# The second low half of each expert on VectorE, and another order of loads and weights around the end of the first expert layer

## What is computed

```python
x = x + _L0_xattn_ref(_layernorm(x), ctx_1024, ctx_1024, mask, wq, wk, wv, wo)  # 16 heads
x = x + _L0_ffn_ref(_layernorm(x), wr, w1, b1, w2, b2)
#     h = _gelu(jnp.einsum('ecd,edf->ecf', xg, w1) + b1[:, None, :])   # 256 -> 1024
#     y = jnp.einsum('ecf,efd->ecd', h, w2) + b2[:, None, :]           # 1024 -> 256
#     wy = y * g[..., None];  summed back to the tokens
x = x + _L1_xattn_ref(_layernorm(x), ctx_1024, ctx_1024, mask_BxS)    # one head of 256, no projections
x = x + _L1_ffn_ref(_layernorm(x), gate_w, w1, w2, w3)                # silu(x w1) * (x w3), then w2
```

## Time and profile before

| | us |
|---|---|
| median of 3 runs | 1095.21 (1092.34 to 1095.92) |
| the profiled execution, its own time | 1098.09 |
| its span, first to last instruction | 1095.9 |
| PE busy in the span | 939.3 (86%) |
| DVE, ACT, POOL busy | 682.5, 545.6, 480.0 |

### The profile page before, as it was taken

The page is one execution under the profiler, slowest core; times in us unless marked ns, Lnnn a source line. Parts: engine busy times, 40 slices in busy tenths (PEclk is TensorE's granted clock), DMA queues, the critical chain, the costliest instruction groups (busy, mean ns, idle before and its releaser), DMA issues. The chain is left out here.

```text
span 1095.9 us, 22844 instructions
## 1 busy us (share of the span) xinstructions
PE 939.3 (86%) x7879; PEld 853.7 (78%) x7879; DVE 682.5 (62%) x1931; ACT 545.6 (50%) x1208; POOL 480.0 (44%) x462
## 2 busy tenths in 40 slices
PE   5889998998899839999999936872799999999997
PEld 4778877877787629898889914662799999999977
DVE  5556565675566557666666625756567777778533
ACT  3778877887788725555555513430234333433221
POOL 2123134142413235666666731356354565456423
PEclk9999998999999859999999968985799999999999
DMA  7878787886576047667766686642543453345101
GB/s 187 172 204 207 184 201 190 222 202 146 148 171 156 28 129 216 166 173 171 172 173 165 137 205 158 179 151 89 191 116 84 114 145 101 101 114 135 18 7 22
DMA packets 110020, 160.22 MB, mean 146 GB/s; under 512 B 11584, under 2 KB 98976, under 8 KB 107968
## 3 DMA queue, kind: packets, MB, share of 16 engines
q1 hardware_dynamic: 95952, 140.16, 48.9%
q0 software_dynamic: 13936, 18.33, 8.3%
HBM read 103.45 MB, written 56.96 MB: 146 GB/s over the span
## 5 line engine op out<-in xcount | busy, mean ns | idle before, releaser
L312 PE MATMUL ps<-XGH,WH 128*128 128x280 f32 (+1 forms) x768 | 223.0, 290 | 16.3 <-ACT GT L836 12.3
L312 PE MATMUL ps<-XGL,WH 128*128 128x280 f32 (+1 forms) x768 | 222.2, 289 | 0.0
L312 PE MATMUL ps<-XGH,WL 128*128 128x280 f32 (+1 forms) x768 | 221.7, 289 | 0.0
L1595 POOL TENSOR_TENSOR HTL<-GT,HTH 128x280 fp32r<-128x280 f32 x128 | 132.9, 1062 | 165.9 <-DVE HTH L1335 165.9
L1207 DVE CUSTOM_DVE_ANT_0 NS<-ps,negm 112x375 f32<-112x375 f32 x256 | 138.0, 545 | 108.4 <-PE ps L418 96.6
L312 PEld LDWEIGHTS ps<-XGH,WH 128*128 128x128 f32 x768 | 148.3, 193 | 21.4 <-ACT GT L836 17.0
L764 ACT ACTIVATE PP<-NS,MN 112x375 f32<-112x375 f32 x256 | 156.4, 611 | 3.2 <-DVE MN L1207 2.7
L312 PE MATMUL ps<-WH,HTH 128*128 128x256 f32 (+1 forms) x536 | 152.4, 284 | 2.0 <-DVE YY L1350 2.0
L426 PE MATMUL ps<-cst,PP 112*125 112x112 f32 x768 | 138.9, 291 | 17.4 <-ACT PP L764 14.5
L312 PE MATMUL ps<-WL,HTH 128*128 128x256 f32 (+1 forms) x536 | 150.5, 281 | 0.0
L312 PE MATMUL ps<-WH,HTL 128*128 128x256 f32 (+1 forms) x536 | 149.9, 280 | 0.0
(11 more groups left out here) (211 smaller groups left out, 1881.7 us busy)
## 6 DMA issues: line engine op xcount, KB each, us to landing
WG<-in_v SPq DMA_DIRECT2D x48, 512.0 KB
KST<-k_scratch SPq DMA_DIRECT2D x48, 376.0 KB, 5.5
WG<-in_w SPq DMA_DIRECT2D x32, 512.0 KB
k_scratch<-KHL SPq DMA_DIRECT2D x64, 188.0 KB
CT<-in_ctx_t SPq DMA_DIRECT2D x32, 375.0 KB, 7.0
xg_scratch<-zero SPq DMA_DIRECT2D x8, 1289.8 KB, 10.3
xg_scratch<-zero SPq DMA_DIRECT2D x16, 586.2 KB, 9.0
XG<-xg_scratch SPq DMA_DIRECT2D x14, 536.0 KB, 3.7
```

Of the source, the lines that this page charges most:

```text
L312: m = e.matmul(out_ap, l, r, start=n == 0, stop=n == len(steps) - 1)
L1595: e.tensor_tensor(HTL[:, f, cols], GT[:, gi % 3, :], HTH[:, f, cols], ALU.subtract).then_inc(hl_pool[layer], 1)
```

## The change

Five edits, all in the order of work or in who does it; what is computed stays the same.

1. **The low half of unit gi = 1 of each expert**, in both layers, is made by DVE: `by_pool(gi)` is true for odd gi except where gi % 16 is 1, and `hl_of` counts by it.
2. **The last block of layer 0** (n = 39, expert 7, c = 4, 48 rows) goes into the first `GT` buffer rather than into `YY`, and no longer waits for the transfer of block 35.
3. **Weights behind rows in layer 0's last expert**: the two pieces of weights 38 and 39 are made after the five blocks on ACT, DVE and POOL, rather than before or between them. Their next loads (pieces 42 and 43, 512 KB each) leave the boundary and go to the start of layer 1's `sp_experts`, behind its first rows.
4. **Contexts ahead of the wait**: SP issues `ctx_t` 2 and 3 and `ctx_n` 1 before it waits for layer 0's adds, and loads the last eight batches of `X` as two pieces of four, with `ctx_n` 2 and 3 between the pieces.
5. **Clears**: expert 3 issues two of the clears, experts 4 to 6 one each, expert 7 none.

```diff
-XLOADS = ((0, 2), (2, 4), (4, 8), (8, B))
+XLOADS = ((0, 2), (2, 4), (4, 8), (8, 12), (12, B))
...
+        def row_block(layer, n):
+            GT, YY = ebufs[layer][5:7]
+            r = rows_of(n % 5)
+            return GT[0:r, 0, 0:D] if (layer, n) == (0, 5 * E - 1) else YY[0:r, n % NY, :]
...
+        def by_pool(gi):
+            return gi % 2 == 1 and gi % 16 != 1
+
         def hl_of(gi):
-            return gi // 2 + 1, (gi + 1) // 2
+            pool = sum(by_pool(i) for i in range(gi + 1))
+            return gi + 1 - pool, pool
...
-                if gi % 2 == 0:
+                if not by_pool(gi):
                     e.wait_ge(hh[layer], gi + 1)
                     e.tensor_tensor(HTL[:, f, cols], g, HTH[:, f, cols], ALU.subtract).then_inc(hl_dve[layer], 1)
...
-                    if n >= NY:
+                    if NY <= n < 5 * E - 1:
                         e.wait_ge(*row_done(0, n - NY))
-                    e.tensor_tensor(YY[0:r, n % NY, :], ps[0:r, 4 + n % 2, 0:D], B2[0:r, u, :], ALU.add).then_inc(y_out[0], 1)
+                    e.tensor_tensor(row_block(0, n), ps[0:r, 4 + n % 2, 0:D], B2[0:r, u, :], ALU.add).then_inc(y_out[0], 1)
...
-                    if c < per - 2 and last:
-                        lo(base + per * ex + 10 + c)
                     rows_done(ex, c)
                     if c < per - 2 and not last:
                         lo(base + per * ex + 10 + c)
+                for c in range(per - 2 if last else 0):
+                    lo(base + per * ex + 10 + c)
```

ACT and POOL have the same move of their weights behind the five blocks. On SP:

```diff
+            if layer == 1:
+                for c in range(2):
+                    sp_chunk(e, 4 * E + 10 + c)
...
                 if layer == 0:
-                    cleared_rest(ex)
+                    for rest in (ex,) if ex < 3 else (3, 4) if ex == 3 else (ex + 1,):
+                        if rest < E:
+                            cleared_rest(rest)
...
                 for c in range(5):
-                    if c < per - 2:
+                    if c < per - 2 and not (layer == 0 and ex == E - 1):
                         sp_chunk(e, base + per * ex + 14 + c)
...
             e.wait_ge(y_mm[0], 5 * E)
             context_n(0)
-            for n in range(5 * E - NY, 5 * E):
-                e.wait_ge(*row_done(0, n))
-            kept(0)
-            kept(1)
             context_t(e, 2)
             context_n(1)
-            kept(2)
             context_t(e, 3)
+            for n in range(5 * E - 1 - NY, 5 * E):
+                e.wait_ge(*row_done(0, n))
+            for i in range(3):
+                kept(i)
             context_n(2)
             kept(3)
             context_n(3)
+            kept(4)
```

More of the change, by code:

```diff
@@ L538, in rows_out @@
                 if c in (0, 2):
-                    by_dve, by_pool = hl_of((ex * 2 + c // 2) * 8 + 7)
-                    e.wait_ge(hl_dve[layer], by_dve)
-                    e.wait_ge(hl_pool[layer], by_pool)
+                    n_dve, n_pool = hl_of((ex * 2 + c // 2) * 8 + 7)
+                    e.wait_ge(hl_dve[layer], n_dve)
+                    e.wait_ge(hl_pool[layer], n_pool)
                 pairs = []
@@ L830, in activated @@
                 if gi >= 3:
-                    by_dve, by_pool = hl_of(gi - 3)
-                    e.wait_ge(hl_dve[layer], by_dve)
-                    if by_pool:
-                        e.wait_ge(hl_pool[layer], by_pool)
+                    n_dve, n_pool = hl_of(gi - 3)
+                    e.wait_ge(hl_dve[layer], n_dve)
+                    if n_pool:
+                        e.wait_ge(hl_pool[layer], n_pool)
                 if layer == 0:
@@ L843, in rows_gated @@
                 r = rows_of(c)
-                y = YY[0:r, n % NY, :]
+                y = row_block(0, n)
                 e.wait_ge(y_out[0], n + 1)
@@ L862, in act_experts @@
                 last = layer == 0 and ex == E - 1
-                for c in range(per - 2 if last else 0):
-                    act_weights_hi(e, base + per * ex + 10 + c)
                 for c in range(5):
@@ L872, in act_experts @@
                         act_weights_hi(e, n)
+                for c in range(per - 2 if last else 0):
+                    act_weights_hi(e, base + per * ex + 10 + c)
                 if between and ex == E - 2:
@@ L1609, in rows_added @@
                     out_offset=bass.IndirectOffsetOnAxis(ap=XG[0:rows_of(c), ex % 2, c, RW_ID:RW_ID + 1].bitcast(I32), axis=0),
-                    in_=YY[0:rows_of(c), n % NY, :], in_offset=None, bounds_check=T - 1, oob_is_err=False,
+                    in_=row_block(layer, n), in_offset=None, bounds_check=T - 1, oob_is_err=False,
                     compute_op=ALU.add).then_inc((d_add0, d_add)[layer][n % NY], 16)
@@ L1618, in pool_experts @@
                     for f in range(8):
-                        if f % 2:
+                        if by_pool((ex * 2 + hf) * 8 + f):
                             halves_lo((ex * 2 + hf) * 8 + f)
```

2 lines of the change are left out of this document (1 added, 1 removed).

## The result

The changed kernel takes 1083.4 us (median; 1081.1 to 1086.4) where the kernel before takes 1095.4 beside it (1092.3 to 1095.9). The ratio of the times is 0.988, with an interval of 0.985 to 0.991: faster by 9 to 16 us. The prediction was 1080, with a range of 1071 to 1090.

What follows compares the result with a forecast made beforehand. PE was taken to wait for ACT in layer 0's experts, then for adds and transferred bytes around the layer boundary. Gains 6.7 + 2.8 + 5.8 = 15.3 us, from the median 1095.21 to 1079.9; range 1071 to 1090.

Steps and rivals of the forecast that it cites:

- Low half: Layer 0's experts: PE's waits at unit 8 go, 0.35 us stays in each of six experts; gain 7.45 us.
- 555.16 plus 0.8: Expert 5, layer 0: POOL's adds end at 555.16, its low half of unit 3 takes 0.8, so ends at 556.0.
- Double clear: Expert 3, layer 0: 1.29 MB more pass while adds are in flight; cost 0.7 us, bounds nothing and about 4.5.
- the bank wait of 0.65: End of layer 0: DVE no longer makes weights ahead of block 35, freeing PE's bank; 0.65 us of PE's time.
- End of layer 0: Weights leave the front of POOL's adds, last block doesn't wait 5.13; X's loads go out earlier; 2.8 us in all.
- Contexts ahead: Second attention: three of nine contexts move ahead of the wait, fewer bytes before batch 4's scores; gain 5.8 us, 3.4 wait stays.
- rival C: Layer boundary: batch 4's context lands first, the hole closes, the last add lands in 3.8; 1074.4 us, chance 0.14.
- A: Layer 0's experts: PE's wait only moves to unit 12, layer 0 gives 2; 1084.6 us, chance 0.16.
- B: Second attention: bound by transfers further on, gives the contexts' gain back; 1085.7 us, chance 0.13.
- D: Layer boundary: four contexts hold SP, X's loads queue behind, batch 4's scores 4.3 late; 1092.8 us or slower, chance 0.04.
- E: Whole kernel: A and B together, the change does next to nothing; 1090.4 us, chance 0.07.

Runs made afterwards that it cites:

- the split: Each ctx_n loaded by two transfers (partitions 0 to 111 and 112 to 124) instead of one: ratio to before 0.9829 in the changed kernel, 0.9873 in the kernel before.
- the two runs on the low half: Kernel before with only unit 1's low half moved to VectorE: ratio to before 0.9938; changed kernel with that edit undone: 0.9928.

## Why the prediction was right, and where not

The forecast of 15.3 us lies inside the measured 9 to 16, at its upper end. Part of that is luck: in the traces layer 0's experts gave 3.6 where the terms have 7.35, and the end of the layer and the second attention gave more than their terms, so that errors of 3 to 4 us stood against each other. And the term of the contexts has about the right number by a reason that doesn't hold. The terms one by one:

**Low half: 7.45 predicted, some 6.5 by the times of two runs, 5.1 and 6.2 in their traces.** The mechanism was right to the unit: the waits at unit 8 are gone, and the next ones stand behind POOL's low halves of units 3 and 5. The size was a little off, since 0.35 was left for each expert and 1.0 stayed. Here is why, in the timelines of ACT, DVE and POOL at the start of expert 2 in the changed kernel:

```profile
479.78 0.88 ACT L847 ACTIVATE GT<-ps,B 128x280 f32<-128x280 f32 x2 [1.74 <-POOL HTL L1606]
...
482.10 1.11 ACT L847 ACTIVATE GT<-ps,B 128x280 f32<-128x280 f32 x2 [1.44 <-POOL HTL L1606]
...
478.03 1.96 DVE L1349 TENSOR_TENSOR HTL<-GT,HTH 128x280 fp32r<-128x280 f32 x1
479.91 0.29 DVE L1346 CAST HTH<-GT 128x280 fp32r<-128x280 f32 x1
...
477.47 1.37 POOL L1618 DMA_INDIRECT x_scratch<-YY,XG  x1 [0.30 <-issue]
478.40 1.27 POOL L1606 TENSOR_TENSOR HTL<-GT,HTH 128x280 fp32r<-128x280 f32 x1
...
480.28 1.70 POOL L1606 TENSOR_TENSOR HTL<-GT,HTH 128x280 fp32r<-128x280 f32 x1 [0.61 <-DVE HTH L1346]
```

The step that failed is "555.16 plus 0.8". The last add in the earlier trace rows runs until 555.60 (554.23 + 1.37), and POOL's first low half behind it ended at 556.4, 0.8 later, with DVE idle. In the changed kernel it is the same: the last add ends at 478.84 (477.47 + 1.37), the low half of unit 3 at 479.67. So that one was due at 556.4 and not at 556.0, which is about the 0.32 that PE waits at unit 10. The second wait has another source. In the same moments DVE made the low half of unit 4, which took 1.96 in place of 0.45; its cast of unit 5 began only at 479.91, and POOL, free at 479.67, waited 0.61 for it (the last row).

The prediction set the Trainium skill's rule (SBUF — State Buffer, Who interferes with whom: a VectorE instruction with two SBUF inputs and a GpSimd instruction that reads SBUF exclude each other) at up to 0.9 for each expert, and then left it out because the new low half falls while POOL issues adds. That was right for the new one in this expert, which took 0.45 beside an add's issue, like the one at 471.28 above, but the rule came in where a later low half of DVE's meets POOL's first. The trace agrees with the rule, and here it was DVE that paid: POOL's low half ended no later behind the add than with DVE idle (0.83 against 0.80). In layer 1's experts little changed (0.7 us less), as predicted.

**Double clear: 0.7 predicted, about 4.5 measured** (217.7 against 213.2 with one clear in each). This is the one term that was plainly mis-sized. The sentence "adds landed nearly in time elsewhere, so I take 0.7" is the step: 4.5 was the bound, from the row with 5.13, and that row was the nearest one in kind, since it too had a clear in flight with an expert's adds. The wait measured was 5.14. The times of that pair differ by only 1.6, uncertain by 4, so the 4.5 are the traces'. Layer 0's experts in sum: 7.35 predicted with the bank wait of 0.65, 3.6 in the trace.

**End of layer 0: 2.8 predicted (0.65 of it inside the experts), 3.3 and 0.6 in the trace, but not for the reasons given.** All that the prediction described took place: no wait of the last block, POOL's adds in a row, the last one ended 4.8 us after PE's end. But undoing edits 2 and 3 lost nothing that can be measured, and putting the clear back into expert 7 didn't delay X's issue either. Either is enough, and the prediction credited the first and counted the second only as bytes. What it left out is a price of edit 4: the contexts ahead of the wait hold the last add back by 1.8 us (4.2 from its issue to X's, 2.4 with them behind).

**Contexts ahead: 5.8 predicted; 4.3 to 5.9 by times, 6.8 from X's issue to the scores of batch 4.** The number holds and its reason doesn't. I divided bytes by the rate of the earlier trace rows and took that rate for a limit of the transfers. Splitting one narrow load raised it from 192 to 224 GB/s, and to 264 with the contexts behind the wait. The gap closed wholly, as in rival C, where 3.4 was to stay, partly because X's first rows landed 2.5 us later and took PE's other work along. That the granted clock stays at 0.50 for 3.4 to 4.5 us behind a gap of 9 us, as three traces show, was in no term; half the work of these microseconds makes it some 2 us more (an estimate). The prediction quoted the Trainium skill (DMA: Bandwidth & Descriptors, Why a DMA increments its semaphore by 16 and not by 1), by which a load over 125 partitions runs on 5 engines and one over 112 on 16, and then used it for a difference of one microsecond. No trace here shows single engines, but two things agree with it. The engines' busy share goes from 0.77 to 1.01 by the split, and the stretches at 0.33 or 0.34, which go with it, are what 5 engines of 16 would give where all give 1.10 (an estimate from that rule and the windows above: 1.10 x 5/16 = 0.34). It should have been asked what the same sentence says of the hole itself.

**The rivals.** A is ruled out by the two runs on the low half. B is partly true: the values' waits nearly doubled, but the whole second attention got shorter. C's first half came true, its second (adds in 3.8) not: 4.2. D had the right place and a small share of its price: issuing the four contexts took SP until 638.91, ahead of the adds' landing, yet X's first rows came 2.5 us later after their issue. E is ruled out with A. The 17.3 of the traces and the 12 of the times differ mostly by the 6 us of the first attention, which came out longer in this execution.

## What to carry to other kernels

A mean rate in GB/s is not a limit until the busy share of the DMA engines stands beside it, in windows short enough to see it rest at a third while PE is about to run dry; the shape of one transfer may be worth as much as a reordering of all. When two edits remove the same wait, price each with the other already made. And a burst of bytes that is moved to "a quiet place" should be priced by the nearest row with a burst, not by the quiet.

## What the runs showed of the hardware

Loads over 125 partitions go with stretches in which the DMA engines' share is 0.30 to 0.37, 27 to 30 us in the second attention against 0.5 to 3 with the split. They hold up others too: in the changed kernel SP stood up to 4.1 us in an issue of `CN` and 4.9 in a store of `X` (1.2 and 0.34 after the split; in the kernel before one issue of `CN` still took 2.7 with it), and the quickest rows of `X` took 5.3 us (2.7 after the split). The indirect adds suffer from bursts, narrow or not: the last one of layer 0 landed 4.2 us after its issue with contexts ahead of the wait, and 4.5 to 5.0 with these split, against 2.4 and 1.2 with the contexts behind; a second clear of 1.29 MB made one land so late that DVE waited 5.14 us. Gaps of 8.5 to 9.3 us on PE left the granted clock at 0.50 until 3.4 to 4.5 us after their end, and one of 3.0 us (the kernel before with the split) until 3.1 us after it. A VectorE low half that meets GpSimd's took 1.96 us instead of 0.45 while GpSimd's beside it ended 0.83 us behind the add before it, against 0.80 with VectorE idle; beside the issue of an indirect transfer VectorE's took 0.45. Whole executions of one kernel differ most in the first attention: 387 to 391 us in two groups and 411 to 417 in a third, and 410 and 416 within one comparison, with granted clocks in it of 0.93 to 0.94 in the first two and 0.89 to 0.91 in the others.
